# Two-layer decoder on one core: in the Mamba stage, five of sixteen input products go from VectorE to GpSimd

## What is computed

```python
def step(h, inp):
    d_t, b_t, c_t, u_t = inp
    dA = jnp.exp(d_t[..., None] * A)
    dBu = d_t[..., None] * b_t[:, None, :] * u_t[..., None]
    h = dA * h + dBu
    y_t = jnp.einsum('bdn,bn->bd', h, c_t)
    return (h, y_t)
```

## Time and profile before

| | us |
|---|---|
| median of 3 runs | 1509.62 |
| lowest and highest | 1507.57, 1511.47 |
| profiled execution | 1518.27 |
| its span | 1516.5 |
| TensorE matmul busy (share) | 1243.7 (82%) |
| VectorE busy | 1040.7 (69%) |
| ScalarE busy | 814.1 (54%) |
| GpSimd busy | 396.7 (26%) |
| mean granted TensorE clock | 0.924 |

### The profile page before, as it was taken

One profiled execution on the slowest core, in us unless ns is written; L12 is line 12 of the kernel. 1 busy time (PEld: TensorE's weight loads), 2 busy tenths in 40 slices (PEclk: granted clock), 3 DMA queues, 4 the chain that ended last, 5 costly groups with the idle time before them and its releaser, 6 DMA issues.

```text
span 1516.5 us, 23285 instructions
## 1 busy us (share of the span) xinstructions
PE 1243.7 (82%) x8400; PEld 807.8 (53%) x8400; DVE 1040.7 (69%) x2162; ACT 814.1 (54%) x2187; POOL 396.7 (26%) x248
## 2 busy tenths in 40 slices
PE   5667779796899889889875777869689987989896
PEld 4323336694566546656631233559656655665563
DVE  5889966114888697477559998721378878755864
ACT  2555513362766266676646653326367635667664
POOL 0136634304000233023010765360400014301400
PEclk9789978897999999998997999789899999999998
DMA  8300001583000010000010000067500000000100
GB/s 306 122 0 1 0 1 66 169 268 102 2 2 2 1 35 22 2 19 17 9 42 0 1 0 1 1 191 247 163 5 2 2 1 14 22 8 7 29 8 14
DMA packets 42179, 72.21 MB, mean 48 GB/s; under 512 B 3793, under 2 KB 27473, under 8 KB 41810
## 3 DMA queue, kind: packets, MB, share of 16 engines
q1 hardware_dynamic: 28242, 56.30, 11.1%
q10 hardware_dynamic: 11776, 10.23, 2.7%
q0 software_dynamic: 2048, 4.20, 0.9%
HBM read 51.19 MB, written 13.24 MB: 42 GB/s over the span
## 4 chain that ended last, share of the span: by engine, by line
PE 46%; DVE 23%; ACT 15%; issue 8%; POOL 3%; DMA 3%; ACTq 1%; SPq 1%; another core or an unknown queue 0%; POOLq 0%; DVEq 0%
DVE scratch L901 6%; PE psum L1339 3%; PE psum L1119 3%; PE psum L1358 3%; DVE scratch L893 3%; PE psum L1133 3%; PE psum L1321 3%; PE psum L1600 3%; ACT scratch L1724 3%; PE psum L1559 2%; PE psum L1334 2%; PE psum L749 2%; PE psum L1632 2%; PE psum L956 2%; PE psum L1448 1%
## 5 line engine op out<-in xcount | busy, mean ns | idle before, releaser
L930 POOL TENSOR_TENSOR scratch<-scratch 128x1024 f32<-128x1024 f32 x64 | 150.5, 2355 | 139.5 <-DVE scratch L901 110.0
L652 POOL TENSOR_TENSOR small<-small,w_const 128x16 f32<-128x16 f32 x32 | 100.8, 3155 | 278.6 <-DVE small L1771 278.6
L901 DVE TENSOR_TENSOR_SCAN scratch<-psum,scratch 128x512 f32<-128x512 f32 x128 | 150.0, 1205 | 5.8 <-ACT psum L822 5.5
L749 PE MATMUL psum<-scratch,w_const 128*128 128x512 f32 x256 | 137.5, 664 | 9.8 <-POOL scratch L930 9.8
L652 POOL TENSOR_TENSOR rstd<-rstd,w_const 128x4 f32<-128x4 f32 x32 | 32.7, 1025 | 399.5 <-DVE rstd L614 385.8
L822 ACT ACTIVATE psum<-scratch,a_neg 128x512 f32<-128x512 f32 x128 | 86.8, 688 | 59.0 <-DVE scratch L901 57.4
L1392 ACT ACTIVATE scratch<-psum,mx 128x256 f32<-128x256 f32 (+1 forms) x256 | 110.7, 458 | 7.9 <-DVE mx L1428 7.9
L1724 ACT ACTIVATE scratch<-psum,mx 128x128 f32<-128x128 f32 x256 | 90.5, 378 | 42.5 <-DVE mx L1812 41.3
L738 PE MATMUL psum<-scratch,cb 96*128 96x512 bf16 x128 | 48.5, 408 | 67.2 <-DVE scratch L893 60.6
L1178 ACT ACTIVATE scratch<-psum,scratch 128x128 f32<-128x128 f32 x240 | 66.9, 377 | 56.8 <-PE psum L1119 45.4
L1261 DVE COPY scratch<-psum 128x128 f32<-128x128 f32 x60 | 17.2, 290 | 113.7 <-PE psum L1133 113.6
(11 more groups left out here) (266 smaller groups left out, 3180.9 us busy)
## 6 DMA issues: line engine op xcount, KB each, us to landing
expert_weights<-in_expert_weights SPq DMA_DIRECT2D x61, 512.0 KB, 15.3
scratch<-scratch ACTq DMA_DIRECT2D x48, 128.0 KB, 2.3
folded_products<-expert_weights SPq DMA_DIRECT2D x8, 512.0 KB, 2.7
folded<-folded_products SPq DMA_DIRECT2D x8, 512.0 KB
w_local<-in_local SPq DMA_DIRECT2D x1, 3122.0 KB
sorted_y<-scratch ACTq DMA_DIRECT2D x12, 256.0 KB, 3.8
scratch<-sorted_x SPq DMA_DIRECT2D x4, 704.0 KB, 6.5
scratch<-in_cross SPq DMA_DIRECT2D x1, 2624.5 KB, 12.9
```

Source lines behind the costliest of these rows:

```text
L652: t.eng.tensor_tensor(v, v, W("const", "neg_half").to_broadcast([P, v.shape[1]]), ALU.pow).then_inc(t.s[done], 1)
L749: ins = pe.matmul(sum_banks[c], ident, t.m.hC[:, 2 * ((n - 1) % 2) + c, :], start=(n == 1), stop=(n == NS))
L901: dve.tensor_tensor_scan(t.m.hs[:, n % 2, c, :], t.ps["dA"], t.m.dBu[n % 2][:, c, :], 0.0, ALU.mult, ALU.add)\
L930: t.eng.tensor_tensor(t.m.hC[:, 2 * (n % 2):2 * (n % 2) + 2, :], t.m.hs[:, n % 2], C, ALU.mult)\
```

## The change

For the states n in `ON_POOL` = (1, 4, 7, 10, 13), VectorE makes no product. ScalarE copies B from the bank to a new SBUF buffer `Bs` (one per lane), which frees the bank, and GpSimd multiplies `du` with `Bs` into the buffer of `dBu` that VectorE would have written, ahead of its product with C of the state before (n - 1). A new semaphore `input_ready` lets VectorE's scan and the next copy of B go. The copy stands ahead of the state's first exponential on ScalarE. GpSimd's product waits for the copy (`v_freed`) and for the scans of state n - 2 (`decay_used`).

The table of turns is made anew for all engines. ScalarE and GpSimd have 10 more steps in each lane; the others have as many as before. Counted from the two tables and the yields, lane 0 being A and lane 1 B:

| | before | after |
|---|---|---|
| TensorE, first pass: steps of B's setup ahead of A's L712 | 34 | 9 |
| VectorE: steps of B's setup ahead of A's last L857 | 20 | 1 |
| VectorE: B's first Mamba step stands behind A's Mamba step | 9th | 28th |
| VectorE: B's first L893 stands behind A's Mamba step | 27th | 39th |
| VectorE: B's last scan stands behind | A's 69th Mamba step | A's 15th cross step |
| TensorE: A's first experts step stands behind | B's 17th cross step | B's 60th, last Mamba step |
| TensorE: B's first block stands behind A's experts step | 21st | 34th |
| TensorE: A's window stage stands behind | all of B's experts | all of B's experts |
| VectorE, second pass: B's first L893 stands behind A's | 21st Mamba step | 21st Mamba step |

In this count a state has three steps on VectorE, and the first L893 of a lane is its 17th Mamba step.

```diff
+ON_POOL = (1, 4, 7, 10, 13)
...
 TURNS = {
     "pe": [
-        5, 34, 4, 1, 1, 4, 2, 3, 1, 1, 3, 1, 5, 2, 3, 3, 3, 3, 3, 3, 2, 1, 1, 2, 5, 3, 3, 3, 2, 1, 1, 2, 2, 2,
+        5, 9, 4, 5, 1, 12, 2, 3, 1, 4, 2, 1, 6, 1, 1, 4, 5, 4, 2, 1, 4, 1, 3, 1, 2, 1, 4, 5, 2, 3, 2, 1, 2, 2,
...
@@ row_buffers
             m.dBu = (m.dBu0, carve(i, 2, T))
+            m.Bs = carve(i, T)
...
@@ mamba_scalar
             for n in range(NS):
+                if n in ON_POOL:
+                    yield
+                    k = len(ON_POOL) * t.row + ON_POOL.index(n)
+                    if k:
+                        act.wait_ge(t.s["input_ready"], k)
+                    act.activation(t.m.Bs, t.v.take(), ACT.Copy).then_inc(t.s["v_freed"], 1)
                 for c in range(NB):
...
                     if c == 0:
-                        t.skip(v=1)
+                        if n not in ON_POOL:
+                            t.skip(v=1)
                         yield
...
@@ mamba_vector
-                if n >= 2:
-                    dve.wait_ge(t.s["decay_used"], NB * (NS * t.row + n - 1))
-                bank = t.v.take().rearrange("p (o z) -> p o z", o=1).to_broadcast([P, NB, T])
-                dve.tensor_tensor(t.m.dBu[n % 2], t.m.du[:, :, :], bank, ALU.mult).then_inc(t.s["v_freed"], 1)
+                if n in ON_POOL:
+                    t.skip(v=1)
+                else:
+                    if n >= 2:
+                        dve.wait_ge(t.s["decay_used"], NB * (NS * t.row + n - 1))
+                    bank = t.v.take().rearrange("p (o z) -> p o z", o=1).to_broadcast([P, NB, T])
+                    dve.tensor_tensor(t.m.dBu[n % 2], t.m.du[:, :, :], bank, ALU.mult).then_inc(t.s["v_freed"], 1)
                 for c in range(NB):
                     yield
                     if c == 0:
-                        dve.wait_ge(t.s["v_freed"], t.v.at)
+                        if n in ON_POOL:
+                            t.w(t.s["input_ready"])
+                        else:
+                            dve.wait_ge(t.s["v_freed"], t.v.at)
...
@@ mamba_pool
             for n in range(NS):
+                if n + 1 in ON_POOL:
+                    yield
+                    if n + 1 == ON_POOL[0]:
+                        t.eng.wait_ge(t.s["delta_ready"], t.row + 1)
+                    t.eng.wait_ge(t.s["v_freed"], t.v.at + 3)
+                    if n >= 1:
+                        t.eng.wait_ge(t.s["decay_used"], NB * (NS * t.row + n))
+                    B = t.m.Bs.rearrange("p (o z) -> p o z", o=1).to_broadcast([P, NB, T])
+                    t.eng.tensor_tensor(t.m.dBu[(n + 1) % 2], t.m.du[:, :, :], B, ALU.mult).then_inc(t.s["input_ready"], 1)
                 t.skip(v=2)
                 yield
```

More of the change, by code:

```diff
@@ L448, in decoder_kernel @@
                      "sorted_stored gathered0 gathered1 "
-                     "squares_ready rms_ready u_ready soft_ready delta_ready parts_ready decay_ready decay_used state_ready states_used "
+                     "squares_ready rms_ready u_ready soft_ready delta_ready parts_ready decay_ready decay_used input_ready state_ready states_used "
                      "sum_filled skip_ready gated_ready gap_ready ratio_ready comb_ready pads_ready "
```

## The result

The changed kernel took 1560.84 us (median of 4 runs, 1556.34 to 1565.67), the kernel before 1508.59 beside it: a ratio of 1.035, 95% interval 1.0315 to 1.0388. The forecast was 1482.6. The profiled execution of after is one of 1556.34 us, span 1554.5, so 38.0 us above the span of before.

The account below looks back on a forecast made before the run. VectorE was taken to set the pace in the second Mamba pass, with no engine the bound throughout; 21 us from the first pass plus 6 from the second, 27 off the median 1509.6, gave 1482.6, range 1466 to 1510.

Parts of the forecast that it names:

- Twenty products at 1.11 us: Mamba passes: 20 products leave VectorE, 11.1 us a pass; 6 us taken as gain for the second, between 0 and 9.6.
- the bound of GpSimd at 97.9 us: Mamba pass: the bound passes from VectorE at 107.5 us to GpSimd, 42 operations of 2.33 us, 97.9 us.
- rivals A to C: Whole kernel: only products count, 1497.6, chance 0.18; collisions in full, 1493.6, 0.10; everything comes back, 1469, 0.12.
- The bank of B that comes free by a short copy: Mamba stage, PSUM: the bank frees earlier, helping TensorE a little; TensorE is not the bound there, so counted as nothing.
- covered while both lanes run: Mamba stage, ScalarE: copies of B at 0.60 us, 6 us a pass, hidden in free time while both lanes run.
- Rival E: Mamba passes: GpSimd's added product waits for a scan, holding the other lane's; pass 119 us, whole 1522.8, slower; chance 0.12.
- Lane 1's last scan at about 206: First Mamba pass: 176 us of VectorE work at 95% full takes 186 us, ending at about 206, against 198.84.
- 45 forecast: First Mamba pass: lane 0's first state starts at 45 us, some 20 us earlier, since fewer setup steps stand ahead.
- the forecast 261: Experts stage: lane 0's first block at 261 us instead of 283.46, since its experts begin at 222 instead of 244.14.
- 21 early: First pass and the experts overlapping it: 21 us saved, products included, between nothing and 31.
- Collisions, 5 us: First pass: VectorE steps with two SBUF inputs meet GpSimd's products, four hits at 1.2 us, 5 us.
- The later stages: Stages after the first pass, such as window and local: the new table changes nothing, zero within 4 us either way.

Follow-up runs that it names:

- e13: As e9, with GpSimd's added product covering 64 of 1024 columns in four of the five states: 1505.43 us, ratio 0.9977.
- e17: As e13, with ScalarE's exponentials from the second state on covering 64 of 512 columns: 1495.33 us, ratio 0.9892.
- e18: The kernel before with exponentials from the second state on covering 64 of 512 columns, nothing else changed: ratio 0.9977.
- e9: As e5, and for the five states TensorE spreads no B and ScalarE copies none: 1523.01 us, ratio 1.0033.
- e1: The change's moved products and copies, but with the table of turns of the kernel before: 1552.87 us, ratio 1.0269.
- e5: As e1, but GpSimd's added product multiplies du with itself and doesn't wait for the copy of B: 1505.84 us, ratio 0.9983.
- e7: As e1, but for the five states B is spread one turn of the PSUM bank earlier and copied there: 1523.0 us, ratio 1.0068.
- e10: As e7, but VectorE makes the five products itself from Bs: 1542.37 us, ratio 1.0158.
- e15: The kernel before with the new table only from the first batches' window stage to the second batches' Mamba stage: ratio 1.0124.

## Why the prediction was wrong, step by step

**Twenty products at 1.11 us, 22.2 us of VectorE, of which most should come back.** The time is right, its worth wrong, and with it the gain went; the next step turned it into a loss. A row of VectorE with no gap in it was read as: whatever leaves VectorE shortens the pass. It only says that nothing else was longer in each place. Behind each product lay an exponential of 0.69 and the way to it and back; uncovered it leaves 0.84 of the 1.11, and a product is worth 0.27, 5.4 us in all (e13, e17, e18). The row was there: VectorE's last scan of the first pass, with no product in front, waited 0.76 us for the exponential.

The Trainium skill, page "Perfetto Trace Analysis", section "Identifying the Most-Contended Engine", says to improve the engine with the highest occupancy first; here that engine was relieved of 11.1 us a pass and the pass gave 2.1 (e13). With this the bound of GpSimd at 97.9 us, the forecast and rivals A to C had no ground.

**The bank of B that comes free by a short copy, "so nothing is counted", and the copy "covered while both lanes run".** This is the term that was put at nothing and cost most. ScalarE's 0.60 us is covered (e9). What I didn't follow was the copy's own start: the bank serves B and C in turn, its spreads stand behind sums, these wait for GpSimd. That ring costs 25 of e1's 134 us (e5), and an earlier spread takes 19.5 us of the pass back (e7). By ratios over the whole kernel: with no copy and next to no product on GpSimd the move is worth 3.5 us, not clear of zero (e13); with the products and early copies it costs 10 (e7), with late copies 41 (e1), and with the new table besides 53 (after).

**Rival E** named the place, an added product waiting in GpSimd's one queue with the other lane behind it, and had 119 us for the pass; it was 121.4. But it had the product wait for a scan, and the rows show it waiting for the copy; and its whole time, 1522.8, is 38 us short, since it too put the later stages at nothing. So the near hit on the pass owes something to luck. It got 0.12 because the table put a step ahead of need; but the step's turn was early, not its data.

**Lane 1's last scan at about 206, from VectorE's conserved work at 95% full.** It fell at 229.9. The first state came at 48.2 (45 forecast), but VectorE was 81% full, not 95. Lane 1 ends the pass, by its own chain of 16 states, and its chain began later: the last step before its first state, after (L884) and before (L882), first and last start:
```profile
L884 DVE TENSOR_TENSOR scratch<-scratch x2: 1210/1217/1224, 46.5 to 118.7; 128x1024 f32<-128x1024 f32 x2
```
```profile
L882 DVE TENSOR_TENSOR scratch<-scratch x2: 1215/1847/2479, 63.1 to 93.5; 128x1024 f32<-128x1024 f32 x2
```
Lane 0 gained 17 us, lane 1 lost 25. Lane 0 then ran alone for 70 us in a chain that one lane can't fill, and from 36 to 50 us TensorE, busy all the time with lane 1's setup, was granted 0.50, the lower level, where before had 1.00 (16 matmuls of one setup step took 3.6 us instead of 2.0). Up to 30 us it had been granted 1.00 in after too, with two waits of 1.1 us for VectorE in between; why the clock fell isn't shown. Lane 0's first expert block (L1122) came at 276.3, where before had 283.46 and the forecast 261, and the window stage began 5.8 us late, not 21 early. Part of the forecast held: behind lane 1's last scan the way to the window stage became 25.3 us shorter, as the forecast had it for blocks that run with less beside them; that these are the reason wasn't tested.

**Collisions, 5 us.** Right in kind and near in size; four hits of 1.2 were forecast, and the rows show two of 2.0. Two of lane 1's steps met GpSimd's products; they took 1.22 without:
```profile
110.89 3.25 DVE L880 TENSOR_TENSOR scratch<-scratch 128x1024 f32<-128x1024 f32 x1
114.17 3.25 DVE L881 TENSOR_TENSOR scratch<-scratch 128x1024 f32<-128x1024 f32 x1
...
110.55 2.51 POOL L939 TENSOR_TENSOR scratch<-scratch 128x1024 f32<-128x1024 f32 x1 [5.04 <-ACT scratch L810]
113.01 3.32 POOL L947 TENSOR_TENSOR scratch<-scratch 128x1024 f32<-128x1024 f32 x1
```
That is 4.1 us. By the rule of the Trainium skill, page "SBUF — State Buffer", section "Who interferes with whom", two SBUF inputs of VectorE and a reading GpSimd exclude each other; the trace agrees, and e10 shows it as a steady state (2.47 for 1.22).

**The later stages, "zero, within 4 either way".** +20.6. I had followed the new table through the Mamba pass and not compared its turns in the window and local stages. e15 shows that they cost the unchanged kernel 19 us by themselves.

## What to carry to other kernels

An engine without a gap isn't a bound that can be lowered by its own time: look in each place for what runs beside the operation to be removed, and look for a row where the operation is missing already. A copy that is short still has a start; follow its input back through every queue until the chain ends or closes, and if it closes, only starting the data earlier helps, not swapping two waits. A remade order of turns is a change of every stage, and is to be compared in every stage, with the products left where they were.

## What the runs showed that I had not expected

TensorE was slower where it had waited. In e1 the clock granted from 850 to 930 us was 0.83 where before has 1.00 in the same stretch (0.98 from 835). In after TensorE was busy 0.39 us from 890 to 894 us, at a granted 1.00, and had 0.57 from 894 to 898: the sums at 894.24, after 3.03 us of waiting for GpSimd, took 3.56 us, and those at 897.86 took 1.88. So the waits of the ring can lengthen the ring. How much of the loss this is wasn't measured.

GpSimd's product of `du` with itself takes 1.89 us, that of `du` with `Bs` 2.35 (e5, e9 against after). `Bs` is also read once for each half of the channels, so which of the two differences it is isn't known.
